# The order of the pieces of a state-space stage: a preference for each kind of piece and batch in its list scheduler

## The reference, cut to what matters

```python
h = x * rsqrt(mean(x * x) + EPS) * rms_w            # x is a layer norm of the residual
x1, g = split(h @ in_W + in_b)                      # 256 channels each
x1 = silu(causal_conv4(x1) + conv_b)
delta, Bm, Cm = split(x1 @ dbc_W + dbc_b)           # 16, 16, 16
delta = softplus(delta @ dup_W + dup_b)             # 256 channels
a, b = exp(delta[..., None] * A), delta[..., None] * Bm[:, :, None, :] * x1[..., None]
h_t = a_t * h_{t-1} + b_t                           # for each channel and each of 16 states
y = silu(g) * einsum('tbdn,btn->btd', h, Cm)
out = y @ out_W + out_b + x
```

## Time and profile before

| | us |
|---|---|
| median of 3 runs | 3945.92 |
| lowest and highest of them | 3945.3, 3949.16 |
| profiled execution: span from its first to its last instruction | 3942.5 |
| profiled execution: its own time, by the median of the runs | 3945.9 (3.4 around the span) |
| state-space stage in that span | 1053.9 to 1675.4 |
| PE, DVE, ACT, POOL busy, share of the span | 82%, 72%, 59%, 31% |
| mean granted clock of TensorE | 0.872 of full |

### The profile page before, as it was taken

How to read it: one execution, slowest core, us unless ns; L and a number is a source line. 1 busy time by engine, 2 the same in 40 slices (tenths; PEclk the granted TensorE clock), 3 DMA queues, 4 the chain that set the end, 5 groups by cost and what they waited for, 6 DMA issues and landing times. The chain is left out here.

```text
span 3942.5 us, 87849 instructions
## 1 busy us (share of the span) xinstructions
PE 3249.7 (82%) x36196; PEld 1488.6 (38%) x36256; DVE 2818.9 (72%) x4293; ACT 2313.5 (59%) x3870; POOL 1237.5 (31%) x1018
## 2 busy tenths in 40 slices
PE   6999999899867677689988888887995676776799
PEld 1222222266411122156533333333453555554445
DVE  8898899587679998887746767655445667656643
ACT  3888888766444555266542566665655564543565
POOL 1100100055436776645533000001004565452100
PEclk7999999999967778799999999998997676656799
DMA  4101010100010010010036011101000000000000
GB/s 102 28 9 28 19 21 5 37 1 2 11 32 16 17 32 16 17 33 1 8 69 82 10 36 33 27 23 53 1 8 4 4 4 4 3 4 3 31 6 17
DMA packets 136019, 84.34 MB, mean 21 GB/s; under 512 B 92386, under 2 KB 107539, under 8 KB 135491
## 3 DMA queue, kind: packets, MB, share of 16 engines
q1 hardware_dynamic: 132870, 74.45, 8.7%
q0 software_dynamic: 2688, 4.20, 0.6%
q10 hardware_dynamic: 64, 0.07, 0.0%
HBM read 46.97 MB, written 18.33 MB: 17 GB/s over the span
## 5 line engine op out<-in xcount | busy, mean ns | idle before, releaser
L989 DVE TENSOR_REDUCE attn_peak_halves<-attn_ps 128x2 f32<-128x1024 f32 x512 | 601.5, 1218 | 58.5 <-PE attn_ps L820 50.7
L942 ACT ACTIVATE attn_weights<-attn_ps 128x512 f32<-128x512 f32 x1024 | 531.0, 601 | 101.4 <-PE attn_ps L848 101.3
L2974 DVE TENSOR_REDUCE sparse_peak<-sparse_ps 128x4 f32<-128x1024 f32 x256 | 309.6, 1223 | 136.3 <-PE sparse_ps L2600 134.5
L1250 POOL TENSOR_TENSOR moe_hidden<-moe_exact,moe_hidden 128x512 f16<-128x512 f32 x256 | 296.7, 1162 | 330.7 <-ACT moe_hidden L1234 322.0
L3672 POOL TENSOR_TENSOR delta_q<-delta_q,delta_weighted 128x512 f32<-128x512 f32 x240 | 324.1, 1377 | 235.4 <-ACT delta_weighted L4066 235.3
L2827 ACT ACTIVATE sparse_weights<-sparse_ps 128x512 f32<-128x512 f32 (+1 forms) x512 | 272.0, 585 | 173.8 <-PE sparse_ps L2667 87.9
L246 PE MATMUL moe_ps<-moe_xT_halves,moe_w_halves 128*128 128x512 f16 x1536 | 363.8, 384 | 9.4 <-DVE moe_w_halves L1267 5.9
L1772 POOL TENSOR_TENSOR mamba_out_c<-mamba_states,mamba_c_rep 128x1024 f32<-128x1024 f32 x128 | 301.4, 2367 | 176.8 <-DVE mamba_states L1839 138.5
L848 PE MATMUL attn_ps<-attn_q_stack,attn_k_stack 50*128 50x512 f16 x1024 | 321.9, 386 | 29.9 <-ACT attn_weights L942 7.1
L246 PE MATMUL ffn_ps<-ffn_layers,ffn_h_halves 128*128 128x512 f16 x1536 | 334.5, 379 | 3.6 <-ACT ffn_gate L3219 3.6
L1558 PE MATMUL mamba_ps<-mamba_stack,mamba_spread 96*128 96x512 bf16 x512 | 196.2, 493 | 157.3 <-ACT mamba_decays L1726 85.7
(11 more groups left out here) (451 smaller groups left out, 6293.4 us busy)
## 6 DMA issues: line engine op xcount, KB each, us to landing
mamba_stack<-mamba_parts SPq DMA_DIRECT2D x96, 128.0 KB, 2.4
sparse_factor<-sp_factor SPq DMA_DIRECT2D x24, 256.0 KB
sp_halves<-sparse_parts SPq DMA_DIRECT2D x8, 512.0 KB, 3.1
ffn_h<-in_h SPq DMA_DIRECT2D x4, 1024.0 KB, 7.9
attn_q_stack<-attn_halves SPq DMA_DIRECT2D x96, 32.0 KB
attn_k_stack<-attn_halves SPq DMA_DIRECT2D x96, 32.0 KB
attn_halves<-attn_hp SPq DMA_DIRECT2D x8, 384.0 KB, 3.1
attn_q_stack<-attn_peak_rows SPq DMA_DIRECT2D x128, 2.0 KB
```

The costliest lines, as they stand in the source:

```text
L942: act.activation(weights[:, at % 2, h, :], use.slot, ACT.Exp).then_inc(*key_act.one())
L989: dve.tensor_reduce(peak_halves[:, turn % PEAKS, keys, at:at + 2], use.slot, AX_X, ALU.max).then_inc(*score_dve.one())
L1250: pool.tensor_tensor(low, exact_sb[:, i % 3, :], hidden[:, i // EB % 3, i % EB, 0, :], ALU.subtract).then_inc(*hidden_low.one())
L2974: dve.tensor_reduce(peak[:, at % PEAKS, unit // 2, 4 * r:4 * r + 4], use.slot.rearrange("p h (a k) -> p (h a) k", a=2), AX_X, ALU.max).the ...
```

## The change

The preference of a piece was one number for its kind (and absent in the state-space stage). It is now looked up by kind and by the piece's first index, the batch. The state-space stage gets an urgency of its own and a table for 25 kinds; the table of the delta stage holds each old number four times.

```diff
+def earlier_by(ahead, piece):
+    return ahead[piece[0]][piece[1] if len(piece) > 1 else 0] if piece[0] in ahead else 0.0
...
-                possible.append((begin - urgency * to_end[piece] - ahead.get(piece[0], 0.0), which, begin, piece, part, filled))
+                possible.append((begin - urgency * to_end[piece] - earlier_by(ahead, piece), which, begin, piece, part, filled))
...
+MAMBA_URGENCY = 0.023035
+MAMBA_AHEAD = {
+    "apply": (-14.7, 13.4, 60.2, -0.2), "bc": (-0.7, 0.3, 0.1, 0.1), "bias": (63.4, 93.5, 15.4, 153.4),
+    "decay": (0.3, -0.5, 0.5, 151.5), "delta": (82.3, 140.8, 153.6, 97.2), "features": (-62.9, 7, 1.8, 0.3),
+    "fill": (14.3, 1.6, 0.6, 0.2), "first_delta": (67.3, 47.6, 44.1, 153.4), "first_rest": (86, 144.4, 177.9, 213.2),
+    "gate": (13.2, 1.4, 0.2, 0.6), "gated": (41.9, 92.8, 73, 25.4), "inputs": (-0.1, -0.1, -0.1, -0.3),
+    "moments": (276.7, 226.4, 140.2, 160.5), "norm_root": (-64.5, 145.2, 111.6, 3.7), "part": (-0.7, -1.3, 0, -0.9),
+    "product": (0.4, 26.1, 21.9, 0.9), "project": (0.3, 1.7, -0.8, -74.5), "rates": (0, 0, 0, -0.2),
+    "rescale": (186.2, 169, 190.5, 175.4), "rest": (227.8, 307.1, 136.5, 125),
+    "restack": (161.2, 111.1, 143.7, 117.8), "scan": (0.4, -0.7, -1.3, -1.1), "silu": (9.5, 18.6, 5.5, 162.1),
+    "softplus": (78.4, 0, 0, 0), "sum": (-1.3, -0.4, -0.5, 0.1)}
...
-    return planned(chains, needs, MAMBA_COST, 0.008, {}, MAMBA_TABLE, banks_for, frees)
+    return planned(chains, needs, MAMBA_COST, MAMBA_URGENCY, MAMBA_AHEAD, MAMBA_TABLE, banks_for, frees)
...
-AHEAD = {"kept": 1.5, "root": 1.5, "sums": 0.5, "norm_root": 0.5, "uw": 0.5, "raw": 2, "hidden": 0.5, "temper": -2, "o_scale": -0.5,
+AHEAD = {
+    "kept": (1.5, 1.5, 1.5, 1.5), "root": (1.5, 1.5, 1.5, 1.5), "sums": (0.5, 0.5, 0.5, 0.5),
...
```

More of the change, by code:

```diff
@@ L3380 @@
 URGENCY = 0.004
-AHEAD = {"kept": 1.5, "root": 1.5, "sums": 0.5, "norm_root": 0.5, "uw": 0.5, "raw": 2, "hidden": 0.5, "temper": -2, "o_scale": -0.5,
-         "values": -0.5, "apply": -2, "silu": -1, "turned": -0.5, "mix": -0.5, "moments": -0.5}
+AHEAD = {
+    "kept": (1.5, 1.5, 1.5, 1.5), "root": (1.5, 1.5, 1.5, 1.5), "sums": (0.5, 0.5, 0.5, 0.5),
+    "norm_root": (0.5, 0.5, 0.5, 0.5), "uw": (0.5, 0.5, 0.5, 0.5), "raw": (2, 2, 2, 2),
+    "hidden": (0.5, 0.5, 0.5, 0.5), "temper": (-2, -2, -2, -2), "o_scale": (-0.5, -0.5, -0.5, -0.5),
+    "values": (-0.5, -0.5, -0.5, -0.5), "apply": (-2, -2, -2, -2), "silu": (-1, -1, -1, -1),
+    "turned": (-0.5, -0.5, -0.5, -0.5), "mix": (-0.5, -0.5, -0.5, -0.5), "moments": (-0.5, -0.5, -0.5, -0.5)}
 def filled_by(piece):
```

## The result

The new kernel takes 3926.34 us (median of 7 runs, 3919.18 to 3937.45) against 3948.87 (7 runs, 3937.93 to 3951.87): ratio 0.9954, 95% interval 0.9941 to 0.9967, so 13 to 23 us faster. The ratio is an estimate over the runs and not the quotient of the two medians, which is 0.9943. The forecast was -14.3 us and 3932.

A forecast was written before the change was run, and what follows sets the result against it. DVE was taken to bound the middle of the state-space stage and a chain through all engines its start; -5.3 (start) - 8 (middle) - 1 (contention) + 0 = -14.3 us, from 3945.9 to 3932, range 3917 to 3948.

The forecast's parts named there:

- What bounds the kernel: State-space stage: DVE bounds the middle, busy 498.98 of 541.4 us; a chain through all engines bounds the 67.1 us start.
- signs of being wrong: Wrong if L1834 and L1839 waits stay 20 us, apply(1) precedes fill, POOL releases scans over 3 us, or other stages move.
- The start, -5.3: Before the first scan: DVE takes the first fill before apply(1), PE fill(0,1) before gate(0,1); -5.3 us, ends -5.4 and 0.
- A chain, and moves as a whole: Start, after the second fill: silu, deltas, softplus, casts, subtractions and restack's DMA all move earlier together by 5.3 us.
- The middle, -8: The 128 scans: of 24.9 us movable DVE waits, softplus stalls mostly go; -8 us, ends -24.9 and +10.2.
- The batch starts stay: Middle: DVE's losses of 4.2 and 5.1 us at the starts of batches 2 and 3 stay.
- Contention, -1: DVE's middle: moving first_rest of batch 0 cuts part of 8.5 us of contention; -1 us, ends -8.5 and +4.3.
- Table loads, 0: ACT in the middle: grouping pieces with foreign tables drops 1.28 us loads, but 278 us of idle covers them; 0.
- the tail, 0: After the last scan: the series is already in order; two DVE adds might move, 0 to -1.3 us, taken as 0.
- Only the start moves, because buffers are too few: Rival for the middle: three bank pairs and decay buffers are too few, order only moves stalls; 3941 us, chance 0.22 including nothing.
- Slower by projections at the low clock: Rival on PE: late fills, gates and softpluses each put 1.8 us on scans; 3957 us with half of them, chance 0.12.
- Nearly everything goes: Rival: DVE's idle is all waits on pieces with slack elsewhere; -5.3 - 20 - 5 = -30 us, 3916 us, chance 0.12.

The follow-up runs named there:

- the second profile: The new kernel profiled again with no edit: stage 605.4 us against 604.9 in its first profile; these runs took 3938.12 us against 3949.86, ratio 0.9975.
- replayed table: New kernel with another table and urgency 0.0227, searched by replaying the orders with traced durations and real waits: stage 597.1 us against 604.9, time 3926.81 us.
- the kernel with the shortest stage: New kernel with the table and urgency 0.0227 found by replaying orders with traced durations: stage 597.1 us, time 3926.81 us, ratio 0.9944.
- the one with the longest: New kernel's table with the old urgency of 0.008: stage 828.8 us, against 621.4 in the kernel before and 604.9 in the new kernel.
- the two replayed kernels: New kernel with the best and second best tables of a search by replay with traced durations: stages 597.1 and 597.4 us, times 3926.81 and 3926.98 us.

## Why the prediction was right, and where not

*What bounds the kernel*: right. The middle is DVE's, and the gain is in its idle time. One of the prediction's own signs of being wrong did come: the stages outside this one moved, by 2.4 and 6.3 us where 1 was allowed. The sign was badly chosen, since such stages differ by more than that between profiles of the same kernel.

*The start, -5.3*: right in mechanism, 2.0 too large in the first profile, 0.7 in the second (-3.3 and -4.6); undoing it cost 4.0. The first fill stands ahead of apply(1), PE's second fill ahead of gate(0,1), as the scores said. The rows:

```profile
1065.75 3.92 DVE L1820 SCALAR_TENSOR_TENSOR mamba_x<-mamba_ps,mamba_conv_w,mamba_x 128x1021 f32<-128x1021 f32 x3 [8.81 <-ACT mamba_x L1684]
...
1069.72 6.61 PE L1575 MATMUL mamba_ps<-mamba_xT,mamba_w_in 128*128 128x512 f32 x8 [3.62 <-DVE mamba_x L1820]
...
1079.85 1.91 ACT L1697 ACTIVATE mamba_x<-mamba_x 128x2048 f32<-128x2048 f32 x1 [2.37 <-DVE mamba_x L1820]
...
1100.21 1.12 ACT L1692 ACTIVATE mamba_gate<-mamba_ps,mamba_b_in 128x1024 f32<-128x1024 f32 x1
1101.22 0.69 ACT L1711 ACTIVATE mamba_c_rep<-mamba_ps,mamba_b_bc 128x512 f32<-128x512 f32 x1
...
1101.79 2.00 ACT L1735 CAST mamba_parts<-mamba_temp 128x1024 bf16<-128x1024 f32 x2
```

The silu begins 27.9 us after the stage's first DMA where it began 33.0 us after it: 5.1 us, nearly all I forecast. "A chain, and moves as a whole" was the step that failed. The last activation of bc's low rank behind the silu came 0.8 us late, behind matmuls that took 5.5 us for 4.5, and the second pair of casts came 1.0 us late, behind a gate and a part of C on ACT, which had more room before. A chain that goes through queues picks up what the queues now hold.

*The middle, -8*: right in mechanism, and the term that was mis-sized. DVE's idle time in the stretch fell by 15.4 us, and some 17 of the 24.9 us of waits went; with the contention below, the stretch as a whole is 13.2 us shorter (11.4 in the second profile). "If ACT enters it with a full store there is no stall" is what the traces show: one finished decay at each of the six softpluses before, three after. "The batch starts stay" failed: 4.2 and 5.1 us became 1.2 us each (1.9 and 1.2 in the second profile). I had reasoned from the gates' own preference and the urgency, one piece at a time. By itself the urgency is worth 2.6 us, and the preferences that I called too small to matter ("under 1 are within what the planner would tie on anyway") are worth more than the whole gain: 22.2 us between 604.9 and 627.1, for all values under 2. They put rates ahead of inputs at 121 of 128 scans, where without them it is 0.

*Contention, -1*: wrong in sign. DVE's busy time rose by 2.2 us. The four L1826 of the middle still collide twice (mean 2286 ns) and the instructions of apply(3) and rescale(3) more than before (L361's mean is 745 ns for 603 ns). The replayed table shows that 4.3 us and more were to be had there.

*Table loads, 0* and *the tail, 0*: right; one or two loads fewer on ACT in the middle (14 for 15 of the decays' own), and 13.3 us of tail in both.

*The rivals.* "Only the start moves, because buffers are too few" falls: with a fourth decay buffer the scans of the kernel before took as long as with three, with another order of the same instructions and the same three they took 13 us less. The rule of the Trainium skill that I had named beside it (Perfetto Trace Analysis, Optimization Strategy), that a repeated gap can mean too few buffers, didn't hold here: 0.5 us for a buffer, 16.5 for an order. "Slower by projections at the low clock" didn't happen: the granted clock of the middle rose from 0.73 to 0.77 of full, a mix of both levels still, and w_in's matmuls did take longer (765 ns on average for 674), but no scan waited for a decay and the multiplications waited less for PE than before. "Nearly everything goes" is what the replayed table comes near to: -24.3 us in the stage, for the -30 I gave.

The sum, -14.3, was within 2.2 us of the stage's -16.5, since the start (2.0) and contention (3.2) were too favourable and the middle's idle time too cautious (7.4: -15.4 for -8). Errors that partly cancelled brought it so near, and not three right terms; that part is luck.

## What to carry to other kernels

When static lists set the order, count from the trace how much finished work lies in the buffer whenever a feeding engine turns to something else. If there is next to none while buffers stand empty, another order of the same instructions can gain and more buffers need not, as here. The totals of what a feeding engine waits for are no measure by themselves: in the kernel with the shortest stage ACT waited 123 us for PE and 44 for a free buffer ahead of its decays, in the one with the longest 364 us for a free buffer. Preferences of such a scheduler are not separable: judge them together, by a replay of the lists with measured durations and the real waits, and put the bounding engine's odd jobs where its feed has a gap. A gain of half a per cent in one stage is best measured by that stage's length in the profile.

## What the runs showed that I had not expected

The stages that this change doesn't touch vary by more than the change is worth: 13.7 us ahead of the stage and 22.1 behind it over 13 profiles. A part of it has a name. In the attention stage, the first, PE's matmuls wait for a DMA (attn_q_stack<-attn_peak_rows). In the new kernel's first profile:

```profile
L852 PE MATMUL attn_ps<-attn_q_stack,attn_k_stack 50*128 50x512 f16 x1024 | 321.2, 385 | 27.0 <-ACT attn_weights L946 7.1 <-ACT attn_hv L918 2.9 <-DMA attn_q_stack<-attn_peak_rows 0.6
```

and in its second:

```profile
L852 PE MATMUL attn_ps<-attn_q_stack,attn_k_stack 50*128 50x512 f16 x1024 | 321.9, 386 | 34.9 <-DMA attn_q_stack<-attn_peak_rows 8.4 <-ACT attn_weights L946 7.1 <-ACT attn_hv L918 2.9
```

7.8 us more of that wait, and the stages ahead are 8.8 us longer; the two replayed kernels show 1.3 and 8.6 us of it, and 1049.3 and 1059.4 us. Over all 13 profiles the wait runs from 0.6 to 12.8 us, and what is left of the stages ahead without it from 1048.0 to 1052.3: 4.3 us of spread in place of 13.7. What makes that DMA late in one execution and not in another was not tried. The variation behind the stage was not traced either.
